# A decoder layer on one core: in cross-attention's second block, one turning goes ahead of the sums and a product of keys and values behind them

## The reference

```
q = x @ Wq.T;  k_raw = context @ Wk.T;  v_raw = context @ Wv.T      # 32 heads of 16
q = rmsnorm(q);  k = rmsnorm(k)                                      # over each head's 16
attn = softmax(einsum('bhnd,bhmd->bhnm', q, k) * 16 ** -0.5)
out = einsum('bhnm,bhmd->bhnd', attn, v)
x = layernorm(x + out)
```

## Time and profile before

| | us |
|---|---|
| median of 3 runs (2381.11 to 2382.21) | 2382.0 |
| the profiled execution, its own time | 2383.09 |
| its span | 2381.4 |
| TensorE busy | 2311.4 (97%) |
| VectorE / ScalarE / GpSimd busy | 1349.4 / 1341.2 / 918.3 |
| TensorE's granted clock, mean | 0.998 |

### The profile page before, as it was taken

The page is one execution under the profiler, slowest core; times in us unless marked ns, Lnnn a source line. Parts: engine busy times, 40 slices in busy tenths (PEclk is TensorE's granted clock), DMA queues, the critical chain, the costliest instruction groups (busy, mean ns, idle before and its releaser), DMA issues. The chain is left out here.

```text
span 2381.4 us, 38050 instructions
## 1 busy us (share of the span) xinstructions
PE 2311.4 (97%) x14970; PEld 1486.9 (62%) x14970; DVE 1349.4 (57%) x2097; ACT 1341.2 (56%) x1687; POOL 918.3 (39%) x610
## 2 busy tenths in 40 slices
PE   9999999999999999999999999999999999999998
PEld 8887544444444444444333556666678899998886
DVE  6677534444343434434332676666775577876785
ACT  4233667677777677667799444444522256665221
POOL 2227664655465643556312343434024112221320
PEclk9999999999999999999999999999999999999999
DMA  6003853456335642546451500002045357876431
GB/s 230 18 18 109 273 166 118 145 186 204 131 101 183 204 152 91 182 133 213 165 162 46 200 1 1 19 1 75 22 138 186 111 193 262 277 257 206 135 116 44
DMA packets 203376, 325.86 MB, mean 137 GB/s; under 512 B 69152, under 2 KB 123680, under 8 KB 203040
## 3 DMA queue, kind: packets, MB, share of 16 engines
q1 hardware_dynamic: 183840, 245.71, 31.1%
q0 software_dynamic: 16336, 72.23, 9.2%
q10 hardware_dynamic: 3024, 5.51, 0.7%
HBM read 237.86 MB, written 95.75 MB: 140 GB/s over the span
## 5 line engine op out<-in xcount | busy, mean ns | idle before, releaser
L1115 ACT ACTIVATE A_c_prob<-c_psum 128x1024 f32<-128x1024 f32 x832 | 786.9, 1030 | 276.4 <-PE c_psum L1380 272.5
L1040 POOL TENSOR_TENSOR E_c_roots<-E_c_roots,c_half 128x32 f32<-128x32 f32 (+1 forms) x70 | 361.3, 5164 | 401.7 <-DVE E_c_roots L1132 401.6
L1391 PE MATMUL c_psum<-A_c_prob,c_vq 128*17 128x512 f32 x3328 | 414.0, 597 | 8.7 <-DVE c_oT L1278 8.5
L143 PE MATMUL c_psum<-E_c_w,E_c_c 128*128 128x512 f32 x1248 | 312.0, 399 | 1.3 <-DVEq L1260 0.7
L143 PEld LDWEIGHTS c_psum<-E_c_w,E_c_c 128*128 128x128 f32 x1248 | 226.7, 188 | 122.0 <-issue 42.3
L1380 PE MATMUL c_psum<-c_qq,c_kq 64*128 64x512 f32 x1664 | 285.8, 436 | 13.9 <-ACT A_c_prob L1115 10.1
L1380 PEld LDWEIGHTS c_psum<-c_qq,c_kq 64*128 64x128 f32 x1664 | 135.9, 185 | 157.1 <-ACT A_c_prob L1115 84.5
L1172 DVE COPY E_c_unit<-c_psum 128x256 f32<-128x256 f32 x89 | 37.8, 424 | 329.2 <-PE c_psum L143 329.2
L2835 PE MATMUL m_psum<-A_m_dn_hi,A_m_a 128*128 128x512 f32 (+1 forms) x570 | 185.8, 394 | 2.4 <-DVE A_m_a L2573 2.3
L1391 PEld LDWEIGHTS c_psum<-A_c_prob,c_vq 128*17 128x17 f32 x3328 | 68.6, 96 | 187.6 <-issue 164.1
L143 PE MATMUL m_psum<-R_g_hi,U_s_up 128*128 128x512 f32 x528 | 170.0, 395 | 0.6 <-DVEq L2554 0.6
(11 more groups left out here) (364 smaller groups left out, 3965.5 us busy)
## 6 DMA issues: line engine op xcount, KB each, us to landing
c_kq<-kd SPq DMA_DIRECT2D x120, 416.0 KB, 5.7
kd<-S_c_t SPq DMA_DIRECT2D x96, 256.0 KB, 2.7
E_c_raw<-in_ctxT SPq DMA_DIRECT2D x89, 256.0 KB, 3.2
qd<-A_c_q SPq DMA_DIRECT2D x32, 512.0 KB, 3.9
c_qq<-qd SPq DMA_DIRECT2D x64, 256.0 KB, 3.2
vd<-A_c_vt SPq DMA_DIRECT2D x104, 136.0 KB, 1.8
c_vq<-vd SPq DMA_DIRECT2D x30, 442.0 KB, 4.9
S_up_raw<-in_sup SPq DMA_DIRECT2D x20, 512.0 KB, 7.0
```

What stands on the lines that cost most here:

```text
L143: mm = pe.matmul(out, a(c), b(c), start=first and i == 0, stop=last and i == len(terms) - 1)
L1040: pool.tensor_tensor(rr[:, unit % RB, 0:n], ms[:, unit % RB, 0:n], half[:, 0:n], ALU.pow).then_inc(s_r, 1)
L1115: act.activation(prob[:, t % PB, 2 * (u % 2):2 * (u % 2) + 2, :], score_banks[u % 3], ACT.Exp, scale=XD ** -0.5).then_inc(s_ex, 1)
L1391: mm = pe.matmul(o_bank[32 * j:32 * j + VW, :], vq[:, q % 2, kt, j, :], prob[:, t % PB, j, :], start=kt == 0, stop=kt == CT - 1)
```

## The change

Block 1 (`TWO`) gets two pieces. The turning T9, which was its fill, is put between its scores and its sums. The planner is told so and then fills the block's ordinary place afresh. The four engines that follow the pieces (SyncE's stores, VectorE's `take`, TensorE's `put`, and GpSimd through `line.items`) take both.

```diff
@@ class Timeline
+    TWO = 1
@@ __init__, after the fills
+        self.normalise[self.TWO - 1].append(self.ahead_of_sums.i)
+
+    def pieces(self, k):
+
+        return ([self.ahead_of_sums] if k == self.TWO else []) + ([self.fill[k]] if self.fill[k] else [])
@@ softmax
             got = None
+            if k == self.TWO:
+                put_at["T", turns[0]] = k
+                self.ahead_of_sums = self.put("T", turns.pop(0))
             placed = lambda key, gap: key in put_at and put_at[key] <= k - gap
@@ SyncE
             for k in range(BLOCKS):
-                piece = line.fill[k]
-                if piece:
+                for piece in line.pieces(k):
                     store(piece)
                     first_quads(piece)
@@ VectorE
+                    if k == line.TWO:
+                        take(line.ahead_of_sums, False, [])
                     piece = line.fill[k]
@@ TensorE
                 for u in range(3 * k, min(3 * k + 3, UNITS)):
                     scores(u)
+                if k == line.TWO:
+                    put(line.ahead_of_sums)
                 for t in line.sums[k][0:1 if line.split_pair[k] else 2]:
                     weighted(t)
```

## The result

The change makes the kernel slower: 2392.3 us (median of 6 runs, 2390.6 to 2395.4) against 2382.2 (6 runs), ratio 1.0043, 95% interval 1.0033 to 1.0053. Timed again with the ninth and tenth experiments it was 2392.1 against 2382.8, 1.0038 (1.0024 to 1.0051). The forecast was 5.2 to 5.4 us slower; 9.3 to 10.1 were measured.

The account below looks back on a forecast made before the run. TensorE, busy 97% of the span, was taken to bound the kernel, so only idle or half-clock time could change. Lost after, 11.85, less 6.5 lost now gave 5.35 us slower: median 2387.4, range 2383.6 to 2391.0.

Parts of the forecast that it names:

- the chain: Blocks 7 to 10: from KV18's end through unit 13's root, the norm's root and scaling to the copy of sums, 13.5 us.
- The sum: Blocks 1 to 17: 11.85 us lost after the change less 6.5 lost now, so 5.35 us slower.
- the new wait: Block 10: TensorE waits 4.8 us before its first sums, for the copy of quad 0's sums.
- Lost now: 6.5: Blocks 1 to 17 before the change: waits for exponentials 1.0, keys 2.3 and 1.0, slower scores 0.5, half clock 1.7 us.
- What moves, blocks 1 and 2: T9 loses at most 0.1 us, KV15 waits 0.6 for bank 7; block 2's 2.3 wait and 1.7 half clock go.
- Block 5: Unit 16's wait for the third part of the keys becomes 1.7 us, not 1.0, plus a store delay of 0.7.
- The delay d: Block 5: later landing of T10's store behind KV15's stores; bounds 0 and 3.6 us, taken as 0.7.
- rival D: Block 5: stores ahead of T10's delay the keys by 3.6 us and the clock falls (1.7): 10 slower, 2392; chance 0.12.
- Blocks 7 to 10: The norm's root falls behind unit 13's root on GpSimd, VectorE's scaling waits, and TensorE waits 4.8 us.
- scaling, up to the copy's start: 1.96: Blocks 7 to 10: VectorE's layer norm scaling, from the norm's root to the copy of quad 0's sums, takes 1.96 us.
- The clock behind it: Behind block 10's wait: half clock costs 1.7 us, bounds 0 and twice the 1.7.
- Blocks 15 and 16: Without fills, 4.6 us of TensorE work for exponentials taking 5.61: waits of 1.0 to 1.1 us, bounds 0.5 and 1.3.

Follow-up runs that it names:

- ninth and tenth experiments: The changed kernel and the kernel before, each profiled and timed once more without any edit: 2392.1 and 2382.8 us.
- experiment 1: The changed kernel with GpSimd's root of the layer norm moved ahead of its work for block 7's piece: 2383.0 us, 1.0003 to the kernel before.
- experiment 2: The kernel before with one more power of 128x32, output unused, ahead of the layer norm's root in GpSimd's list: 2387.8 us, 1.0022 to before.
- experiment 4: Experiment 1's kernel with the turning T10 also put ahead of block 2's sums in TensorE's order: 2382.7 us, 0.9999 to the kernel before.
- experiment 5: Experiment 4's kernel with SyncE issuing KV15's context load and stores behind T10's store and its loads: 2380.8 us, 0.9994 to the kernel before.
- Experiment 8: The changed kernel with GpSimd waiting behind the norm's root until VectorE's scaling is done, holding back the split: 2387.8 us, 1.0030 to the kernel before.
- experiments 2 and 3: The kernel before with an unused power ahead of the norm's root, 128x32 in the former, 128x16 in the latter: 2387.8 and 2385.5 us.

## Why the prediction was wrong

The direction, the place and the chain were right: experiment 1 takes the chain away and the loss with it, experiment 2 puts a like one into the old order and the loss comes there. The sizes were wrong. The sum was 3.2 us short on the first pair of traces, and the time lay outside its range. Four terms failed. The scaling measured 3.15 us instead of 1.96. The half clock behind the new wait cost 2.6 and 2.0 instead of 1.7. Half clock in block 5 was put at nothing and cost 1.6 in one trace of two. "Lost now: 6.5" was 4.15 in the second trace of the kernel before. The first is explained by an experiment; what decides the falls of the clock stays open.

- **What moves, blocks 1 and 2**: as forecast. T9 waits 0.15, KV15 0.53 (0.6 forecast), unit 8 nothing; block 2's half clock goes (granted clock 1.00 from 260 to 265 us).
- **Block 5**: the wait is 1.77 and 1.23 instead of 2.4, since the third part of the keys comes no later behind T10 than before. From T10's start to unit 16's it is 10.79 and 10.25 us in the changed kernel, 10.73 and 10.59 before. The delay d, by the prediction's own measure what the wait has over 1.7, was 0.07 and nothing, not 0.7. That error made up for 0.6 us of the others, which is luck. The order ahead of T10's store does matter as soon as T10 is early: its store lands in 4.7 us in experiment 4 and in 1.9 in experiment 5. The Trainium skill, "DMA: Bandwidth & Descriptors", section "Queues, rings and completion order", has each DMA engine consume a ring's descriptors in order; the two numbers agree with that. They would also come out so if transfers under way merely shared the engines' time, and no run tells the two apart.
- **A fall of the clock in block 5** stood only in rival D. It came in the first trace (0.86 in the sums and 0.70 in the product, 1.6 us) and not in the second. The sum forecast a wait of 2.4 us there and no fall behind it, though the prediction's own row shows one behind a wait of 2.30 and the same row served to price block 10. The term was left out without a reason.
- **Blocks 7 to 10, the term "scaling, up to the copy's start: 1.96"**. It measured 302.13 - 298.98 = 3.15. The row I took it from has GpSimd idle beside it. Here GpSimd went straight on to the split for KV21, which ran beside VectorE's scaling. Experiment 8 shows it: with the split held back, 1.92 and a wait of 4.83. Beside a root the scaling isn't slowed (1.91, experiment 1). The first trace of the kernel before already had a sign. There VectorE's multiplication of a unit takes 1.79 us beside the split that stands in the earlier trace rows, and 0.68 alone:

```profile
286.71 1.28 POOL L1033 TENSOR_TENSOR E_c_c<-E_c_raw,E_c_c 128x512 fp32r<-128x512 f32 x1
...
286.75 1.79 DVE L1138 TENSOR_TENSOR E_c_unit<-E_c_unit,E_c_roots 128x512 f32<-128x512 f32 x1
```

- **The clock behind it**: 1.71 in the sums, 0.45 in the turning, 0.46 in the scores, 2.6 us against 1.7 forecast; 2.0 in the second trace.
- **Blocks 15 and 16**: waits of 0.15 and 0.42 and slower scores around them. From the first scores of block 15 to those of block 17 it is 330.03 - 324.31 = 5.7 us against the 4.6 of work, so 1.1, as forecast.
- **The sum** with these, on the first pair: 5.35 - 0.6 (block 5's wait) + 1.6 (its half clock) + 1.2 (scaling) + 0.9 (clock in block 10) = 8.45; measured 8.55.
- **"Lost now: 6.5 us"** was true of one execution. In the other it was 1.0 + 1.08 + 1.57 + 0.5 = 4.15, without the 1.7 of half clock. So the forecast set 2.35 us against the loss that this execution doesn't have to give. Nor is that rare. In the four traces with the old order of blocks and its waits for keys (before, again, experiments 2 and 3) these waits add up to 2.65 to 3.33 us, and half clock follows in two. On the second pair this, and not block 5's fall, is the largest part of the miss: 5.35 + 2.35 - 1.2 (block 5's wait) + 1.2 (scaling) + 0.3 (clock) = 8.0, and 8.1 were measured.

Behind block 17 the medians have 1 to 1.5 us more than the 8.1 to 8.6. Some of it is half clock behind waits that both kernels have. In the first trace of the changed kernel it comes in self-attention, behind waits of 0.60 and 0.91 us that stand in the kernel before as 0.61 and 0.91. Changed kernel, then before:

```profile
1471.50:1475.00 3.50, 3.01 (x8) 2.43 (x9) 1.09 (x2) 0.30 (x1) 2.55 (x3) 0.65 0.00 0
```

```profile
1463.00:1466.50 3.50, 3.13 (x16) 2.40 (x16) 0.98 (x2) 0.27 (x2) 2.46 (x2) 1.00 0.00 0
```

The second trace of the changed kernel lacks it. Why the medians are further apart than the traces of experiments 9 and 10 stays open.

## What to carry to other kernels

Work that is placed by a fixed block number ("behind the piece in block 7") changes its neighbours when a planner moves the pieces: list, for each engine, what now stands ahead of such a place, and who waits behind it. A duration read from a row holds for what the other engines did beside it; look at that before it goes into a chain. A wait that varies between executions should enter the sum as a range, and one trace doesn't show which waits do.

## What the runs showed of the hardware

- VectorE's scaling of four 128x512 tiles took 3.12 us in both traces in which GpSimd's copy and subtraction of 128x512 ran beside it. It took 1.91 or 1.92 with nothing beside it, and 1.91 with a power of 128x32 beside it (experiment 1), which itself took 5.66 instead of 5.43.
- VectorE's multiplication of 128x512 took 0.68 alone and 1.79 when it began just behind GpSimd's subtraction (286.75 and 286.71 us, kernel before). When it began first, it kept its 0.68 and the subtraction took 1.70 instead of 1.28 (280.78 and 280.90 us, changed kernel).
- The clock behind idle stretches of TensorE: all four of 4.4 to 6.0 us were followed by half clock, which cost the next work up to 2.6 us. Of the waits over 1.05 us for keys or for the copy in blocks 2, 5 and 10, those of 2.30, 2.27, 1.77 and 1.57 us were, and those of 1.95, 1.57, 1.48 (twice), 1.34, 1.31, 1.23, 1.17 and 1.08 were not. The same length of 1.57 went both ways, and in experiment 8 half clock came in block 1 behind waits of at most 0.42, so length alone doesn't decide.
